# An attention unit's pieces in a new order on TensorE, VectorE, ScalarE and GpSimd

## The reference, cut to what matters

```python
q, k, v = (silu(conv4(x @ w)) for w in (wq, wk, wv))       # 128 columns a head
k_unit = k / (norm(k) + EPS)
err = v - k @ proxy_w                                      # its norms feed a small MLP
beta_fast, beta_slow, lam, amp_fast, amp_slow = gates(mlp(features))
decay = exp(-exp(A_log) * softplus(dt_bias) * amp)         # per channel and token
for t in range(512):                                       # fast and slow
    S = S * decay[t]
    S = S + outer(k_unit[t] * beta[t], v[t] - k_unit[t] @ S)
    o[t] = q[t] @ S
o = lam * o_fast + (1 - lam) * o_slow
out = (o / rms(o) * onorm_w * sigmoid(x @ g1_w @ g2_w + g2_b)) @ wo
```

## Time and profile before

| | |
|---|---|
| median of 3 runs | 4288.86 us |
| the profiled execution, its span | 4301.73 us, 4299.9 us |
| PE, PEld busy | 4000.7 us (93%), 2486.6 us (58%) |
| DVE, ACT, POOL busy | 3105.3 us (72%), 2296.8 us (53%), 933.6 us (22%) |
| granted TensorE clock, mean | 0.96 of full speed |

### The profile page before, as it was taken

How to read it: one execution, slowest core, us unless ns; L and a number is a source line. 1 busy time by engine, 2 the same in 40 slices (tenths; PEclk the granted TensorE clock), 3 DMA queues, 4 the chain that set the end, 5 groups by cost and what they waited for, 6 DMA issues and landing times. The chain is left out here.

```text
span 4299.9 us, 179869 instructions
## 1 busy us (share of the span) xinstructions
PE 4000.7 (93%) x76866; PEld 2486.6 (58%) x76866; DVE 3105.3 (72%) x5135; ACT 2296.8 (53%) x6321; POOL 933.6 (22%) x1927
## 2 busy tenths in 40 slices
PE   7999999999999999999999999757879789999998
PEld 4667767767676676767667676522333334444443
DVE  4788888888888888888888887478999991212221
ACT  4577776676676667676676766444344331111110
POOL 1333333333333333333233333100000000000000
PEclk8999999999999999999999999778989899999999
DMA  2222222222221212212122221142323332000000
GB/s 76 65 60 71 65 69 68 58 76 66 63 68 59 77 52 75 70 56 78 57 70 70 63 71 49 41 148 72 94 83 96 92 121 89 29 1 30 0 20 10
DMA packets 133721, 277.31 MB, mean 64 GB/s; under 512 B 21004, under 2 KB 62496, under 8 KB 129472
## 3 DMA queue, kind: packets, MB, share of 16 engines
q1 hardware_dynamic: 132784, 265.60, 20.2%
q10 hardware_dynamic: 144, 0.20, 0.0%
HBM read 235.07 MB, written 30.67 MB: 62 GB/s over the span
## 5 line engine op out<-in xcount | busy, mean ns | idle before, releaser
L420 PE MATMUL a_pb<-a_x_t,a_w_qkv 128*128 128x512 f32 x1536 | 844.0, 641 | 15.5 <-DMA a_x_t<-in_x_t 8.2
L1318 DVE TENSOR_TENSOR a_nq<-a_nq,a_tot 128x1024 f32<-128x1024 f32 x320 | 392.8, 1227 | 133.9 <-PE a_pb L451 85.2
L1281 DVE SCALAR_TENSOR_TENSOR a_acc<-a_pb,a_taps,a_acc 128x511 f32<-128x511 f32 (+2 forms) x576 | 425.5, 739 | 31.1 <-ACT a_acc L866 17.4
L2119 PE MATMUL m_p_y<-m_h,k_ident_sb 128*128 128x512 f32 x512 | 285.4, 710 | 130.7 <-DVE m_h L2356 130.7
L2830 DVE TENSOR_TENSOR a_x_t<-f_gate,f_pb 128x512 f32<-128x512 f32 x128 | 88.0, 687 | 383.1 <-ACT f_gate L2754 383.1
L2754 ACT ACTIVATE f_gate<-f_pb 128x512 f32<-128x512 f32 x132 | 78.8, 597 | 411.7 <-PE f_pb L2695 275.4
L420 PEld LDWEIGHTS a_pb<-a_x_t,a_w_qkv 128*128 128x128 f32 x1536 | 241.1, 192 | 99.0 <-issue 67.4
L451 PEld LDWEIGHTS a_pb<-a_nq,a_ks 128*32 128x32 f32 x20480 | 214.3, 111 | 143.3 <-issue 112.8
L2350 DVE TENSOR_TENSOR_SCAN m_h<-m_da,m_h 128x2048 f32<-128x2048 f32 x64 | 283.1, 4424 | 17.7 <-ACT m_da L2262 12.4
L1718 POOL COPY a_apt<-a_apt_fine 32x256 f32<-32x256 f32 x256 | 100.5, 393 | 882.4 <-DVE a_apt_fine L1336 857.8
L2119 PEld LDWEIGHTS m_p_y<-m_h,k_ident_sb 128*128 128x128 f32 x512 | 112.7, 228 | 295.1 <-DVE m_h L2356 161.9
(11 more groups left out here) (332 smaller groups left out, 8841.6 us busy)
## 6 DMA issues: line engine op xcount, KB each, us to landing
a_rows<-rows SPq DMA_DIRECT2D x192, 512.0 KB, 3.9
a_amp_sums<-amp_sums SPq DMA_DIRECT2D x64, 508.0 KB, 3.7
attn_o<-a_o_out SPq DMA_DIRECT2D x64, 256.0 KB, 2.7
m_b_rows<-ssm_bc SPq DMA_DIRECT2D x64, 256.0 KB, 3.7
m_c_rows<-ssm_bc SPq DMA_DIRECT2D x64, 256.0 KB, 4.5
k_big<-attn_o SPq DMA_DIRECT2D x16, 1024.0 KB, 8.3
a_w_qkv<-in_w_qkv SPq DMA_DIRECT2D x48, 256.0 KB, 3.2
k_big<-in_w_gu SPq DMA_DIRECT2D x3, 1536.0 KB, 13.3
```

Source lines behind the costliest of these rows:

```text
L420: mm = nc.tensor.matmul(pb[:, V_BANK if i == P_V else KQ_BANK], w_qkv[:, i, k], x_t[:, k, b * T:(b + 1) * T], start=(k == 0), stop=(k == D ...
L1281: last = nc.vector.scalar_tensor_tensor(acc[:, i, d:T], src[:, 0:T - d], taps[:, i, 3 - d:4 - d], acc[:, i, d:T], ALU.mult, ALU.add)
L1318: last = nc.vector.tensor_tensor(part, part, spread(blocks, list(part.shape)), ALU.mult)
L2119: nc.tensor.matmul(p_y[:, et], ident[:], h[:, (b * DS + n) % 3, et], start=(n == 0), stop=(n == DS - 1), skip_group_check=True).then_inc(s ...
```

## The change

Every engine's `slot` is rewritten: the same pieces with the same operands, in another order. On VectorE, ScalarE and GpSimd most pieces move from `late` to `later`, which is `s.at(-2)`; that names the unit and adds one slot at the end (`UNITS + 5`), while GpSimd's row of instructions stays the same. Two waits stand at other pieces: that for `g1_kept` moves to `gate_logits` of the first unit, and `gate_low` waits itself for its part of x. The pieces of the first and last slots (`unsure`, `gate_low`, `ssm_first`) move too.

```diff
 def over_units(slot):
-    for n in range(-3, UNITS + 4):
+    for n in range(-3, UNITS + 5):
         slot(Slot(n))
...
                 def gate_logits(s):
+                    if s.n == 3:
+                        pe.wait_ge(g1_kept, B)
                     pe.wait_ge(g2_in, s.head_due(-3, 16, 16))
...
                 def gate_low(b):
+                    pe.wait_ge(x_in[b], 16)
                     if b >= 2:
...
                 def slot(s):
                     late = s.at(-1)
+                    if late.has(-1):
+                        recur_odd(late, 0)
+                    if late.has(0):
+                        products(late, 2)
+                    if late.has(1):
+                        turn_rows(late)
                     if late.has(0):
                         x_fine_sum(late, 1)
...
```

More of the change, by code:

```diff
@@ new lines, in slot @@
+                    if late.has(0):
+                        products(late, 3)
+                    if late.has(0):
+                        w_fine_sum(late, 2)
+                    if s.n == 0:
+                        unsure(3)
+                    if late.has(-1):
+                        recur_u(late, 1)
+                    if late.has(-3):
+                        gate_logits(late)
+                    if s.n == UNITS + 1:
+                        ssm_first(FIRST_DBL)
+                    if late.has(-1):
+                        recur_odd(late, 1)
@@ new lines, in slot @@
+                    if late.has(0):
+                        products(late, 4)
+                    if late.has(0):
+                        x_fine_sum(late, 2)
+                    if s.n == UNITS + 1:
+                        ssm_first(FIRST_DT)
+                    if late.has(3):
+                        project(late, 3, P_K, 0)
+                    if late.has(3):
+                        project(late, 3, P_K, 1)
+                    if late.has(-1):
+                        recur_even(late, 2)
@@ L745, in slot @@
[L745 to L752, removed]
+                        ssm_first(FIRST_DT + 1)
+                    if late.has(2):
+                        gram_kq(late)
+                    if s.n == UNITS + 2:
+                        ssm_first(FIRST_DT + 2)
+                        ssm_first(FIRST_DT + 3)
@@ new lines, in slot @@
+                    if s.n == 1:
+                        keep_g(3)
+                    if later.has(0):
+                        copy_w(later, 4)
+                    if s.n == 1:
+                        log_sum(2)
+                    if later.has(1):
+                        exp_e1(later)
+                    if later.has(-1):
+                        copy_u(later, 3)
+                    if s.n == UNITS + 1:
+                        ssm_first(1)
+                    if later.has(2):
+                        log_err(later)
@@ L1615, in slot @@
[L1615 to L1618 removed]
+                        decay_nq(late, 5)
                 nc.vector.memset(apt[:], 0.0)
@@ L1755, in slot @@
                     late = s.at(-1)
+                    later = s.at(-2)
+                    if later.has(2):
+                        make_feats(later)
+                    if later.has(1):
+                        reset_y(later)
                     if late.has(1):
```

502 lines of the change are left out of this document (226 added, 276 removed).

## The result

The changed kernel takes 4802.88 us at the median of four runs (4786.30 to 4819.47), against 4292.21 us of the kernel before run beside it. The ratio is 1.1197, with a 95% interval of 1.1158 to 1.1237. The forecast was 4322 us. All the time is in the attention.

The account below looks back on a forecast made before the run. TensorE's row of pieces was taken as the attention's bound. Terms of -1.25, +0.4, +0.65 and +0.8, less about 0.1 overlap, gave +0.5 us a unit, +31 us over some 62 units, +2 at the ends: 4322 us, range 4240 to 4390.

Parts of the forecast that it names:

- Term 1: TensorE's own work: fewer runs of whole pieces, each with an uncovered weight load of 0.21 us; -1.25 us a unit.
- Term 3: Recurrence behind exp_tot: TensorE newly waits at recur_u (3) and recur_odd (3); +0.65 us a unit.
- Term 4: TensorE's turn_feats waits for GpSimd, whose spread_y copies are obstructed by VectorE's operations; +0.8 us a unit.
- Term 2: TensorE's instruction blocks: tiled pieces put together outrun the fetch of 256 instructions; +0.4 us a unit, bounds +0.1 and +0.8.
- the 1.3 us between are stalls: Old order: the gap between TensorE's 40.05 us unit and the mean 41.37 us was taken as instruction-block stalls.
- Rival B: GpSimd loses the port to VectorE thrice, turn_feats waits 2 us; +1.65 us a unit, 4391 us; chance 12%.
- a unit over 42.5 us: Sign: a mean unit longer than this would point to Rival B, or to instruction fetches delayed beside SP's row transfers.
- the waits at lines 516, 528 and 645: Sign: TensorE waits a few tenths at 516 and 528 once a unit, and before 645 for GpSimd's a_feats.
- The copies of line 1733: Sign: more than one in four of these GpSimd copies would last over 1 us.
- PE's busy time: Sign: TensorE's busy time in the same work must fall by some 80 us in all.

Follow-up runs that it names:

- a_first_tap: Changed kernel with GpSimd's make_feats ahead of spread_y, VectorE's invert ahead of grow (4) and ScalarE's tap of K ahead of exp_tot: 4497.28 us.
- a_first_tap_split: a_first_tap with four pairs of tiled pieces on TensorE taken apart by whole pieces: 4490.32 us.
- a_first_tap_u: a_first_tap with ScalarE's copy_u of chunk 3 ahead of exp_e1: 4623.50 us.
- a_rows16: a_first_tap with SP's transfers of rows filling 16 of 128 partitions from the seventh slot on, the other decays left out: 4519.41 us.
- a_filler: Changed kernel with 13 matmuls of 128x128, their result overwritten, run by TensorE ahead of turn_feats' wait for GpSimd: 4691.62 us.
- a_pe_l1p: a_first_tap_u with the wait for ScalarE's log_err moved from GpSimd's make_feats to TensorE's turn_feats: 4474.09 us.
- a_feats_late: Changed kernel with turn_feats moved back on TensorE behind w_64_sum and a Q step, and hidden_1 behind products (1): 4546.07 us.
- a_pe_l1p_split: a_pe_l1p with two pairs taken apart (turn_v ahead of turn_rows, w_fine_sum 2 behind gate_logits): 4468.46 us.
- b_feats_up: Kernel before the change with turn_feats alone moved up, directly behind xy_32_sum: 4567.87 us.
- a_u_q: a_first_tap_u with TensorE's w_64_sum behind a Q step and y_64_sum behind products (1): 4627.03 us.

## Why the prediction was wrong

The sign and the places were right. The size was off by 480 us. By its own steps:

- Term 1, fewer uncovered weight loads, has its sign but not its size: 0.7 to 0.9 us a unit by the units at full clock, against 1.25 (the 1.43 of the table is too much, as said there). The fastest such unit has TensorE busy for 39.23 us (a_first_tap), where 38.8 was forecast. The price of a run holds: four pairs taken apart in a_first_tap_split bring the 39.55 us to 40.44, 0.22 us each. What takes back the rest isn't known.
- Term 3, the recurrence, held: 21.1 us at line 516 and 20.8 us at line 528 over 63 units are 0.67 us, against 0.65. a_first_tap and a_first_tap_u confirm both causes.
- Term 4 failed in size. Its own working gave 1.3 to 2.3 us if three copies meet VectorE (its numbers, 4.8 and 2.2 against 5.8, make 1.2). I took 0.8, "between none and the row of before", though the text said that the obstructing operations had moved exactly beside the copies. It measured 2.41. The sum had the products of `make_feats` at their undisturbed length: both are slow now, about 1 us longer each, and so are two copies, 0.8 us each. With these 3.6 us on the 4.8 the path is 8.4 us against 5.8, a wait of 2.6.
- Term 2 failed in size: +1.53 against +0.4, outside its bound of +0.8. Stalls at dense places grow faster than the shortfall under 3.6 us that I laid over the orders: by 3.2, not by 1.3. The base was wrong too: "the 1.3 us between are stalls" measures the mean unit from the fastest one, and the rows with "issue" give 0.71. That the stalls are waits for a block holds. In the trace after, at each of the 80 block edges with a pause over 1 us, TensorE went on 1.2 to 1.5 us (80% of them) after the instruction queue's packet had landed. These packets took no longer than the others (1.13 against 1.07 us at the median), but set out later, 2.4 us after the edge before it against 1.1. What makes a packet set out late stays open; a_rows16 speaks against SP's transfers. By the Trainium skill's "mostly hidden" (Runtime: NRT & Kernel Launch, Instruction fetch mechanics) the term would be none; here 141.5 us stand open.
- The step that failed most: the largest part had no term. The sum charged each wait its own length, and the profile of before had a clock of 1.00, so the clock wasn't asked about. The half clock gave more than 4 of the 8.19 us (4.81 by the table, 4.1 to 4.3 by the units at full clock). a_filler and a_pe_l1p show it from two sides: work in place of a wait, and a wait taken away, both bring the clock back. The trace of before had the sign. Two stalls, of 0.80 and 1.18 us, stand ahead of 20 us at half clock:

```profile
2652.01 0.25 PE L472 MATMUL a_pb<-a_x_fine,a_apt_fine 32*32 32x16 f32 x9 [0.80 <-issue]
2653.44 0.65 PE L472 MATMUL a_pb<-a_x_fine,a_apt_fine 32*32 32x16 f32 x55 [1.18 <-issue]
```
```profile
2655.00:2675.00 20.00, 17.33 (x456) 0.50 0.11 42
```

Rival B had the mechanism and 2 us; with the clock's part of the table it would have been 6.5 us a unit. Of the signs named, a unit over 42.5 us and the waits at lines 516, 528 and 645 came true. Two did not. The copies of line 1733 (1734 now) are over 1 us in one of 256, not in more than one in four, since those of line 1730 and the products are the slow ones. And PE's busy time didn't fall by 80 us but rose by 213, through the clock.

Of the 510 us, a_feats_late gives back 257, and a_pe_l1p_split, which has no wait at `turn_feats`, 334. What stays, 2.6 us a unit over before, is by its rows: 1.1 more of block stalls (1.85 against 0.71), 1.7 more of waits (line 528 alone 0.9), 0.3 of half clock, less 0.5 of work. Whether another order of the same pieces could keep the 0.7 to 0.9 us of work without waits isn't shown.

## What to carry to other kernels

Before a reorder is priced, list the engine's full-clock stretches and ask what each new wait does to the clock: here a wait of 1 to 3 us on TensorE around the small MLP cost 0.6 to 2.3 times its length again, at most, by the half clock column (b_feats_up 1.8 us beside 2.8, a_u_q 2.4 beside 1.04). A handover is to be timed by its durations beside the neighbours that it will have (GpSimd beside VectorE's operations with two inputs in SBUF), not by its best ones, and with every signal that it waits for, as `log_err` in b_feats_up. And a wait that is taken away sends the engine to the next late result: look for that one first, as a_first_tap_u showed.

## What the runs showed of the hardware

- GpSimd's operations of 4 elements take 0.20 us alone and 1.18 to 1.25 us beside VectorE's tensor_tensor of 128 x 1024 with both inputs in SBUF.
- In the attention TensorE's granted clock falls to 1.2 GHz, for a few to some 20 us, around waits and stalls of 1 to 3 us: in the kernel after, 84 of 91 such stretches begin with an idle time of over 1 us close by. The same length costs differently by place: 2.6 us at `turn_feats` gave 9.9 us of half clock after the change and 2.8 us gave 5.4 in b_feats_up. Shorter waits seldom did: those at line 528, 0.3 us on average, in 2 of 57 cases, and 0.9 us in a_pe_l1p_split in 1 of 62.
- At half clock pieces of the whole array take up to twice as long (two matmuls of line 420 2.08 us against 1.12), tiled ones 1.4 times (line 451: 1.08 against 0.76).
- Two tiled pieces of 128 instructions in a row stall at a block's edge by up to 2.8 us, and row transfers of an eighth of the size don't relieve that. The pause ends 1.4 us (median) after the block's packet has landed.
